# The attention mask of a four-layer graph kernel: TensorE's mask products or an addition on VectorE

## The chip, the cores and the metric

The kernel runs on one core of one Trainium2 chip. Its engines are TensorE (PE, with its weight loads as PEld), VectorE (DVE), ScalarE (ACT), GpSimd (POOL) and SyncE (SP, which issues DMAs here). The metric is the device time of one execution in microseconds (us), lower is better.

## The reference

Input are 128 graphs of 64 nodes with 256 features (`x`, float32) and one 64x64 adjacency matrix `adj` of zeros and ones. Four graph layers follow one another, each with a residual and a layer norm: x = layernorm(x + layer(x)).

- Layer 0 is graph attention of one head, masked by multiplication with `adj`.
- Layer 1 is a graph convolution, `adj @ x @ weight + bias`.
- Layer 2 is attention with 8 heads of 32, a projection and an inner layer norm. Its core:

```python
attn = jnp.einsum('bhnd,bhmd->bhnm', q, k) * scale
attn = jnp.where(attn_mask[None, None] == 0, -jnp.inf, attn)
attn = jax.nn.softmax(attn, axis=-1)
o = jnp.einsum('bhnm,bhmd->bhnd', attn, v)
```

- Layer 3 is a gated recurrent layer of three steps, each with two aggregations over the graph, gates z and r, a candidate, and an update of h.

## The kernel before, in words

The 8192 rows are cut into 16 units of 512 rows (8 graphs, four tiles of 128 rows; two graphs share a tile). The kernel is a software pipeline over all layers, written out by hand. Each engine has one stream, `body(i)`, that runs for i from -4 to 16 (2 to 11 as a loop on the chip, the rest written out). In pass i the engine works on layer 3 of unit i, on most of layer 2 of unit i + 1, on layer 1 and the first part of layer 2 of unit i + 2, and on layer 0 of unit i + 3. The order inside `body` is the order on the engine; a `Signal` is a semaphore on which one engine waits for a count of another's work. Nothing reorders the parts.

PSUM is two groups of four banks of 512 float32: `X` holds gates and candidates of layer 3 (`RZ` and `HV`), `Y` all of the layers 0 to 2. Large products are made of three float32r products each (`matmul3`, L109 to L111). In the trace all banks are called `banks`; `l_prob` is `l2_prob`, `l_mx` is `l2_mx`, `l_qk` is `l2_qk`, and `l_h`, `l_r`, `l_rh_hi` and `l_rh_lo` belong to layer 3. `l_qk` also receives the transposed probabilities.

The change is in the masked softmax of layer 2, at the start of each pass:

- TensorE, `l2_mask` (L592): it waits for the four copies of q and k to SBUF (`l2_qk_ready`, ScalarE, L908) and for the copies of v (L847). Then, for each of four banks, one bf16 product of the identity with the broadcast mask writes 0 or -3e38 into all 512 columns.
- TensorE, `l2_score` (L603): 128 small products of 32x64 accumulate onto the mask. Heads lie in four groups of 32 rows, and each group has a bank.
- VectorE, `l2_max` (L1290) and `l2_shift` (L1298): four times a maximum over the 64 nodes of each head, read from the bank, and four times the bank less that maximum, written to `b.prob` in SBUF.
- ScalarE, `l2_exp` (L928): four exponentials, in place, in `b.prob`. The first waits for all four shifts.
- TensorE, `l2_turn_prob` (L614): sixteen transposes, four for each exponential. They write into the banks of the scores.
- ScalarE, `l2_take_prob` (L847, out `l_qk`): four copies to SBUF. TensorE, `l2_attend` (L629): 64 small products with v, each quarter after its copy.

Between the scores and the transposes TensorE has five parts of layer 3, `l3_u` twice, `l3_r` twice and `l3_w` once: 30 products of 512 columns. Between transposes and attend it has `l3_diff(i, 0, 0)`, six more. After attend come `l3_w(i, 0, 1)` and `l3_candidate(i, 0, 0)`, which needs `b.rhs` (L1148, `l_rh_lo`) from VectorE. VectorE does the eight softmax instructions first in its pass, right behind `l1_add_bias` (L1256) of the pass before, and then `l3_reset` (L1381). ScalarE has `l3_reset(i, 0, 0)` (L971) before the exponentials and `l3_reset(i, 0, 1)` and a copy (`l3_high_rh`) between the copies of the probabilities. The last TensorE part of a pass is `l3_turn` (L727), which transposes the new h (L1405). `l1_residual` is L1268, `l0_residual` is L1236.

```python
def body(i):                 # VectorE, start of a pass
    l2_max(i + 1, 0)
    l2_max(i + 1, 1)
    l2_shift(i + 1, 0)
    l2_max(i + 1, 2)
    l2_shift(i + 1, 1)
    l2_max(i + 1, 3)
    l2_shift(i + 1, 2)
    l2_shift(i + 1, 3)
    l3_reset(i, 0, 0)
```

Of the kernel before, what the change touches and what calls it, by code (L numbers as in the profile page):

```python
# [7 lines left out]
BF16 = mybir.dt.bfloat16  # L8
ALU = mybir.AluOpType
# [3 lines left out]
GRAPHS, NODES, DIM = 128, 64, 256  # L13
P = 128
PER_TILE = P // NODES
TILES = 4
GROUP = TILES * P
UNITS = GRAPHS * NODES // GROUP
CH = DIM // P
HEADS, HD = 8, 32  # L20
ROWS = P // HD
# [12 lines left out]
class Signal:  # L34


    def __init__(self, p, name, per):
        self.sem, self.per = p.sem(name), per
# [34 lines left out]
class Program:  # L73
    def __init__(self, nc, a, out, stack):
        self.nc, self.a, self.out, self.stack = nc, a, out, stack
        self.taken = []
        self.ps = [stack.enter_context(nc.psum_tensor(f"banks{s}", [P, TILES, BANK], F32)) for s in (0, 1)]
        sb = self.sb
        self.ident = sb("ident", [P, P])
        self.ident_bf = sb("ident_bf", [P, P], BF16)  # L80
        self.adj_t = sb("adj_t", [P, P])
        self.adj2 = sb("adj2", [P, NODES])
        self.mask_bias = sb("mask_bias", [P, NODES], BF16)
        self.nan_rows = sb("nan_rows", [P, 1])
        self.same_graph = sb("same_graph", [P, P])
        self.ident2 = sb("ident2", [P, NODES])
        self.eps = sb("eps", [P, TILES])
        self.minus_half = sb("minus_half", [P, TILES])
        self.const_ready = self.sem("const_ready")

    def sb(self, name, shape, dt=F32, stack=None):
        return (stack or self.stack).enter_context(self.nc.sbuf_tensor(name, shape, dt))
# [33 lines left out]
def constants(p, block, own, first_load):  # L126
    nc = p.nc
# [32 lines left out]
    @block.vector  # L160
    def _(dve):
        links = Links(dve, chain)
        dve.wait_ge(loaded, 64)
        dve.wait_ge(made, 1)
        for b in range(PER_TILE):
            q = slice(b * NODES, (b + 1) * NODES)
            nc.vector.memset(p.same_graph[q, q], 1.0)
        nc.vector.tensor_copy(p.ident_bf[:, :], p.ident[:, :])
        nc.vector.tensor_tensor(p.ident2[:, :], p.ident[:, 0:NODES], p.ident[:, NODES:P], ALU.add)
        nc.vector.tensor_scalar(p.mask_bias[:, :], p.adj2[:, :], 0.0, MASKED, ALU.is_equal, ALU.mult)  # L170

        links.link(nc.vector.tensor_scalar(hits[:, :], p.adj2[:, :], 0.0, None, ALU.not_equal))
        links.link(nc.vector.reduce_sum(count[:, :], hits[:, :], AX.X))
        links.link(nc.vector.tensor_scalar(count[:, :], count[:, :], 1.0, None, ALU.min))
        links.link(nc.vector.reciprocal(count[:, :], count[:, :]))
        links.link(nc.vector.tensor_scalar(p.nan_rows[:, :], count[:, :], 0.0, None, ALU.mult))
        dve.wait_ge(turned, 1)
        links.link(nc.vector.tensor_copy(p.adj_t[:, :], p.ps[0][:, 0, 0:P]))
        links.link(nc.vector.tensor_copy(hits[:, 0:1], p.nan_rows[:, :]))
        nc.vector.memset(count[:, :], 0.0).then_inc(p.const_ready, 1)  # L180
# [140 lines left out]
class Signals:  # L321
    def __init__(self, p):
        one = lambda name, per: Signal(p, name, per)
# [15 lines left out]
        self.l2_turned, self.l2_hi, self.l2_lo = one("l2_turned", CH), one("l2_hi", CH), one("l2_lo", CH)  # L339
        self.l2_qk_done, self.l2_qk_ready = one("l2_qk_done", 2 * CH), one("l2_qk_ready", 2 * CH)  # L340
        self.l2_v_done, self.l2_v_staged, self.l2_v_swapped = one("l2_v_done", 1), one("l2_v_staged", 2), one("l2_v_swapped", 32)
        self.l2_scored, self.l2_maxed, self.l2_shifted = one("l2_scored", ROWS), one("l2_maxed", ROWS), one("l2_shifted", ROWS)
        self.l2_exp, self.l2_prob_turned, self.l2_prob_t = one("l2_exp", TILES), one("l2_prob_turned", TILES), one("l2_prob_t", TILES)
        self.l2_pv_done, self.l2_inv, self.l2_o = one("l2_pv_done", TILES), one("l2_inv", 2), one("l2_o", 1)
# [20 lines left out]
def fused(p, block, w, b, s, norms, src, dst):  # L365
# [6 lines left out]
    nc = p.nc  # L372
    X, Y = p.ps
# [90 lines left out]
    def _(pe):  # L464
# [120 lines left out]
            ins.then_inc(s.l2_v_done.sem, 1)  # L585

        @within
        def l2_mask(u):
            pe.wait_ge(*s.l2_qk_ready.at(u, 2 * CH))
            pe.wait_ge(*s.l2_v_staged.at(u, 2))  # L590
            for r in range(ROWS):
                nc.tensor.matmul(Y[:, r, :], p.ident_bf[:, :],  # L592
                                 p.mask_bias[:, :].unsqueeze(1).to_broadcast([P, TILES * CH, NODES]),
                                 start=True, stop=False, skip_group_check=True)

        @within
        def l2_score(u, t):
            for c in range(CH):
                for n in range(PER_TILE):
                    for r in range(ROWS):  # L600
                        q = slice(t * P + n * NODES, t * P + (n + 1) * NODES)
                        col = (t * CH + c) * NODES
                        ins = nc.tensor.matmul(  # L603
                            Y[n * NODES:(n + 1) * NODES, r, col:col + NODES],
                            b.qk[r * HD:(r + 1) * HD, c, q], b.qk[r * HD:(r + 1) * HD, CH + c, q],
                            start=False, stop=True, skip_group_check=True)
                        if (t, c, n) == (TILES - 1, CH - 1, PER_TILE - 1):
                            ins.then_inc(s.l2_scored.sem, 1)

# [125 lines left out]
            aggregate(HV[:, k, :], b.h_tok, k).then_inc(s.adj_done.sem, 1)  # L735

        def body(i):
            l2_mask(i + 1)
            l2_score(i + 1, 0)
            l2_score(i + 1, 1)  # L740
            l2_score(i + 1, 2)
            l2_score(i + 1, 3)
            l3_u(i, 0, 0)
# [363 lines left out]
    def _(dve):  # L1107
# [39 lines left out]
        def lower(parts, k, bank):  # L1147
            return nc.vector.tensor_tensor(parts[1][:, k, :], bank, parts[0][:, k, :].bitcast(F32), ALU.subtract)  # L1148
# [134 lines left out]
        def l2_low(u, k):  # L1283
            dve.wait_ge(*s.l2_hi.at(u, k + 1))
            lower(b.late, k, Y[:, 2 + k, :]).then_inc(s.l2_lo.sem, 1)

        @within
        def l2_max(u, r):
            dve.wait_ge(*s.l2_scored.at(u, r + 1))
            nc.vector.tensor_reduce(b.mx[:, r, :], Y[:, r, :].rearrange("p (n j) -> p n j", j=NODES),  # L1290
                                    AX.X, ALU.max).then_inc(s.l2_maxed.sem, 1)

        @within
        def l2_shift(u, r):
            dve.wait_ge(*s.l2_maxed.at(u, r + 1))
            by_bank = b.prob[:, :, :, :].rearrange("p t (c r) j -> p t c r j", c=CH)
            m = b.mx[:, r, :].rearrange("p (t c) -> p t c", t=TILES).unsqueeze(3).to_broadcast([P, TILES, CH, NODES])
            nc.vector.tensor_tensor(by_bank[:, :, :, r, :], Y[:, r, :].rearrange("p (t c j) -> p t c j", t=TILES, c=CH),  # L1298
                                    m, ALU.subtract).then_inc(s.l2_shifted.sem, 1)

        @within
# [126 lines left out]
        l3_offset = within(lambda u: l3.take_offset(dve, u))  # L1428

        def body(i):  # L1430
            l2_max(i + 1, 0)
            l2_max(i + 1, 1)
            l2_shift(i + 1, 0)
            l2_max(i + 1, 2)
            l2_shift(i + 1, 1)
            l2_max(i + 1, 3)
# [149 lines left out]
```

## Time and profile before

| | |
|---|---|
| median of three runs | 1490.17 us (1487.84 to 1492.82) |
| the profiled execution | 1487.55 us |
| its span, first to last instruction | 1485.5 us |
| instructions | 26652 |
| mean granted TensorE clock | 0.961 of full speed |
| data moved by DMA | 34.62 MB, 23 GB/s on average |

The profile is of one execution. A row of the timeline has the start in us from the span's start, the duration, the engine, the line of the kernel, the operation with output and inputs, the shape, a count where neighbours of one kind are merged, and in brackets the idle time of the engine in front of it with what ended it. TensorE's products are pipelined, so the duration of one is longer than the distance to the next start.

### The profile page before, as it was taken

The page shows a single profiled execution, that of the slowest core. Times are in us where ns is not written, and L with a number is a line of the kernel's source. Part 1 is how long each engine was busy: PE and PEld are TensorE (multiplying, and loading weights), DVE is VectorE, ACT ScalarE, POOL GpSimd, SP SyncE. Part 2 cuts the span into 40 slices and gives each one's busy share as a digit, 9 for nine tenths or more (in the row PEclk, how much of TensorE's full clock was granted, in tenths as well). Part 3 has the DMA queues.
Part 4 walks back from the last instruction along what each step waited for, and adds up shares of the span by engine and source line. Part 5 has one row for each costly group of instructions (what it writes and reads, how often), then busy time and mean ns, then how long its engine had stood idle before and what let it go on. Part 6 is the DMA issues. An engine that isn't in the chain of part 4 may idle for free.

```text
span 1485.5 us, 26652 instructions
## 1 busy us (share of the span) xinstructions
PE 1365.8 (92%) x10357; PEld 1153.5 (78%) x10357; DVE 1058.4 (71%) x2366; ACT 794.1 (53%) x1450; POOL 146.5 (10%) x196
## 2 busy tenths in 40 slices
PE   3566799999999999999999999999999999999885
PEld 2455688888888888888888888888888888878674
DVE  3455587777778787777778787777778787757444
ACT  1342455566656555565656555565656555555433
POOL 4300001110001011110001011110001001100000
PEclk8677799999999999999999999999999999999998
DMA  4000100000000000000000000001000000001000
GB/s 136 15 22 1 36 1 23 29 15 23 15 21 28 21 28 21 28 14 23 12 21 28 21 28 21 28 14 28 7 21 28 22 29 8 29 1 37 1 29 15
DMA packets 54661, 34.62 MB, mean 23 GB/s; under 512 B 34896, under 2 KB 51536, under 8 KB 54608
## 3 DMA queue, kind: packets, MB, share of 16 engines
q1 hardware_dynamic: 52800, 29.43, 6.7%
q0 software_dynamic: 1248, 3.94, 0.8%
q8 instruction: 36, 0.59, 0.2%
q10 hardware_dynamic: 560, 0.52, 0.1%
q14 instruction: 17, 0.14, 0.0%
HBM read 12.92 MB, written 8.39 MB: 14 GB/s over the span
## 4 chain that ended last, share of the span: by engine, by line
PE 67%; DVE 17%; ACT 8%; issue 4%; POOL 2%; DMA 0%; ACTq 0%; SPq 0%; POOLq 0%; DVEq 0%
PE banks L109 16%; PE banks L110 15%; PE banks L111 15%; PE banks L485 8%; PE banks L480 3%; PE banks L537 2%; PE banks L629 2%; ACT y L284 2%; PE banks L614 2%; PE banks L603 2%; DVE l_stats L256 2%; DVE l_r L1399 1%; ACT banks L982 1%; ACT l_qk L908 1%; DVE late_lo L1148 1%
## 5 line engine op out<-in xcount | busy, mean ns | idle before, releaser
L971 ACT ACTIVATE l_r<-banks,bias_r 128x512 f32<-128x512 f32 x96 | 65.9, 686 | 223.3 <-PE banks L111 223.3
L270 POOL TENSOR_TENSOR l_rstd<-l_mv,eps 128x4 f32<-128x4 f32 x48 | 28.3, 589 | 949.3 <-DVE l_mv L264 949.3
L988 ACT ACTIVATE banks<-banks,bias_h 128x512 f32<-128x512 f32 x96 | 63.3, 659 | 59.7 <-PE banks L111 59.6
L1148 DVE TENSOR_TENSOR l_rh_lo<-l_r,l_rh_hi 128x512 fp32r<-128x512 f32 x96 | 66.0, 688 | 36.6 <-ACT l_rh_hi L847 36.3
L1399 DVE SCALAR_TENSOR_TENSOR l_r<-banks,l_r 128x512 f32<-128x512 f32 x96 | 66.0, 687 | 32.1 <-ACT banks L982 29.2
L1381 DVE SCALAR_TENSOR_TENSOR l_r<-l_r,l_h 128x512 f32<-128x512 f32 x64 | 43.6, 682 | 55.4 <-ACT l_r L971 55.4
L284 ACT ACTIVATE y<-l_sum,l_offset,l_rstd 128x256 f32<-128x256 f32 x128 | 70.6, 591 | 19.0 <-DVE l_offset L278 19.0
L109 PE MATMUL banks<-l_rh_hi,u_hi 128*128 128x512 f32 x192 | 78.2, 408 | 0.0
L485 PE MATMUL banks<-adj_t,y 128*128 128x128 f32 x512 | 67.7, 282 | 10.9 <-ACT y L284 9.9
L982 ACT ACTIVATE banks<-banks,bias_z 128x512 f32<-128x512 f32 x96 | 63.5, 662 | 25.9 <-PE banks L111 25.9
L110 PE MATMUL banks<-l_rh_hi,u_lo 128*128 128x512 f32 x192 | 75.7, 394 | 0.0
L111 PE MATMUL banks<-l_rh_lo,u_hi 128*128 128x512 f32 x192 | 75.6, 394 | 0.0
L485 PEld LDWEIGHTS banks<-adj_t,y 128*128 128x128 f32 x512 | 62.4, 196 | 15.0 <-ACT y L284 10.6
L485 PE MATMUL banks<-adj_t,l_htok 128*128 128x128 f32 x512 | 67.2, 287 | 3.7 <-ACT l_htok L847 3.7
L485 PEld LDWEIGHTS banks<-adj_t,l_htok 128*128 128x128 f32 x512 | 62.4, 199 | 9.8 <-ACT l_htok L847 9.8
L908 ACT ACTIVATE l_qk<-banks 128x512 f32<-128x512 f32 x64 | 38.3, 599 | 51.9 <-PE banks L111 50.1
L727 PE MATMUL banks<-ident,l_h 128*128 128x128 f32 x384 | 50.9, 276 | 13.2 <-DVE l_h L1405 13.2
L847 ACT ACTIVATE l_rh_hi<-l_r 128x512 fp32r<-128x512 f32 x96 | 60.7, 632 | 4.0 <-DVE l_r L1381 4.0
L284 ACT ACTIVATE y<-l_sum,l2o_offset,l2o_rstd 128x256 f32<-128x256 f32 x64 | 33.3, 591 | 52.3 <-DVE l2o_offset L278 52.3
L1381 DVE SCALAR_TENSOR_TENSOR l_r<-l_r,f_h 128x512 f32<-128x512 f32 x32 | 22.2, 692 | 53.0 <-ACT l_r L971 52.4
L284 ACT ACTIVATE l_res<-l_res,l_offset,l_rstd 128x256 f32<-128x256 f32 x64 | 36.2, 596 | 41.8 <-DVE l_offset L278 41.8
L727 PEld LDWEIGHTS banks<-ident,l_h 128*128 128x128 f32 x384 | 44.1, 142 | 17.7 <-DVE l_h L1405 15.8
(238 smaller groups left out, 4370.9 us busy)
## 6 DMA issues: line engine op xcount, KB each, us to landing
x_tok<-in_x_dram SPq DMA_DIRECT2D x16, 512.0 KB, 3.8
l_res<-y SPq DMA_DIRECT2D x16, 512.0 KB, 2.9
out_dram<-l_res SPq DMA_DIRECT2D x16, 512.0 KB, 2.9
l_vpair<-l_vstage SPq DMA_DIRECT2D x32, 128.0 KB, 3.1
w_raw<-in_L_gnn_w_w_dram POOLq DMA_DIRECT2D x3, 512.0 KB, 9.7
qkv_raw<-in_L_gnn_w_qkv_dram POOLq DMA_DIRECT2D x1, 768.0 KB, 7.4
u_raw<-in_L_gnn_u_w_dram POOLq DMA_DIRECT2D x2, 256.0 KB, 9.7
l_w_raw<-in_L_gnn_W_dram ACTq DMA_DIRECT2D x1, 256.0 KB, 4.8
```

The costliest lines, as they stand in the source:

```text
L109: nc.tensor.matmul(out, w[0], x[0], start=first, stop=False, skip_group_check=True)
L110: nc.tensor.matmul(out, w[1], x[0], start=False, stop=False, skip_group_check=True)
L111: return nc.tensor.matmul(out, w[0], x[1], start=False, stop=last, skip_group_check=True)
L284: return self.p.nc.scalar.activation(y[:, t, :], z[:, t, :], ACT.Identity, scale=self.rstd[:, t:t + 1], bias=self.offset[:, t:t + 1])
L485: ins = nc.tensor.matmul(bank[:, columns(t)], tokens[:, t, k * P:(k + 1) * P], p.adj_t[:, :], start=True, stop=True)
L727: ins = nc.tensor.transpose(RZ[:, n, t * DIM + k * P:t * DIM + (k + 1) * P], b.l3_h[:, k, columns(2 * n + t)], p.ident[:, :])
L971: nc.scalar.activation(b.r[:, m, :], RZ[:, m, :], ACT.Tanh, scale=0.5, bias=w.biases["r"][:, m:m + 1]).then_inc(s.r_ready.sem, 1)
L982: nc.scalar.activation(RZ[:, m, :], RZ[:, m, :], ACT.Tanh, scale=0.5, bias=w.biases["z"][:, m:m + 1]).then_inc(s.z_ready.sem, 1)
L988: nc.scalar.activation(HV[:, m, :], HV[:, m, :], ACT.Tanh, bias=w.biases["h"][:, m:m + 1]).then_inc(s.hv_ready.sem, 1)
L1148: return nc.vector.tensor_tensor(parts[1][:, k, :], bank, parts[0][:, k, :].bitcast(F32), ALU.subtract)
L1381: nc.vector.scalar_tensor_tensor(b.r[:, m, :], b.r[:, m, :], 1.0, h_before(step)[:, m, :], ALU.add, ALU.mult).then_inc(s.rh.sem, 1)
L1399: nc.vector.scalar_tensor_tensor(b.r[:, m, :], RZ[:, m, :], 1.0, b.r[:, m, :], ALU.add, ALU.mult).then_inc(s.step.sem, 1)
```

## The change

The mask goes from TensorE to VectorE, in all units. The four mask products go; the wait in front of them stays as `l2_wait_to_score`, and the score products start their banks' regions themselves. VectorE gets `l2_add_mask`: for each bank it adds the mask, broadcast over tiles and heads and now held in float32, and writes the sum to `b.prob`. Maximum and shift then read `b.prob` instead of the bank. The bf16 identity goes from the set-up. VectorE's written order has the four additions between the maxima.

```diff
-        self.ident_bf = sb("ident_bf", [P, P], BF16)
-        self.mask_bias = sb("mask_bias", [P, NODES], BF16)
+        self.mask_bias = sb("mask_bias", [P, NODES])
...
-        nc.vector.tensor_copy(p.ident_bf[:, :], p.ident[:, :])
...
+        self.l2_masked = one("l2_masked", ROWS)
...
-        def l2_mask(u):
+        def l2_wait_to_score(u):
             pe.wait_ge(*s.l2_qk_ready.at(u, 2 * CH))
             pe.wait_ge(*s.l2_v_staged.at(u, 2))
-            for r in range(ROWS):
-                nc.tensor.matmul(Y[:, r, :], p.ident_bf[:, :],
-                                 p.mask_bias[:, :].unsqueeze(1).to_broadcast([P, TILES * CH, NODES]),
-                                 start=True, stop=False, skip_group_check=True)
...
                             b.qk[r * HD:(r + 1) * HD, c, q], b.qk[r * HD:(r + 1) * HD, CH + c, q],
-                            start=False, stop=True, skip_group_check=True)
+                            start=True, stop=True, skip_group_check=True)
...
         def body(i):
-            l2_mask(i + 1)
+            l2_wait_to_score(i + 1)
...
+        by_bank = b.prob[:, :, :, :].rearrange("p t (c r) j -> p t c r j", c=CH)
+
+        @within
+        def l2_add_mask(u, r):
+            dve.wait_ge(*s.l2_scored.at(u, r + 1))
+            over = p.mask_bias[:, :].unsqueeze(1).unsqueeze(1).to_broadcast([P, TILES, CH, NODES])
+            nc.vector.tensor_tensor(by_bank[:, :, :, r, :], Y[:, r, :].rearrange("p (t c j) -> p t c j", t=TILES, c=CH),
+                                    over, ALU.add).then_inc(s.l2_masked.sem, 1)
+
         @within
         def l2_max(u, r):
-            dve.wait_ge(*s.l2_scored.at(u, r + 1))
-            nc.vector.tensor_reduce(b.mx[:, r, :], Y[:, r, :].rearrange("p (n j) -> p n j", j=NODES),
+            dve.wait_ge(*s.l2_masked.at(u, r + 1))
+            nc.vector.tensor_reduce(b.mx[:, r, :].rearrange("p (t c) -> p t c", t=TILES), by_bank[:, :, :, r, :],
                                     AX.X, ALU.max).then_inc(s.l2_maxed.sem, 1)
...
-            nc.vector.tensor_tensor(by_bank[:, :, :, r, :], Y[:, r, :].rearrange("p (t c j) -> p t c j", t=TILES, c=CH),
+            nc.vector.tensor_tensor(by_bank[:, :, :, r, :], by_bank[:, :, :, r, :],
                                     m, ALU.subtract).then_inc(s.l2_shifted.sem, 1)
...
         def body(i):
+            l2_add_mask(i + 1, 0)
+            l2_add_mask(i + 1, 1)
             l2_max(i + 1, 0)
+            l2_add_mask(i + 1, 2)
             l2_max(i + 1, 1)
             l2_shift(i + 1, 0)
+            l2_add_mask(i + 1, 3)
             l2_max(i + 1, 2)
             l2_shift(i + 1, 1)
             l2_max(i + 1, 3)
```

## Rows read from the trace of the kernel before

**Rows 1.** The page, busy time of each engine, share of the span, instructions.

```profile
PE 1365.8 (92%) x10357; PEld 1153.5 (78%) x10357; DVE 1058.4 (71%) x2366; ACT 794.1 (53%) x1450; POOL 146.5 (10%) x196
```

**Rows 2.** Stretches: one pass; columns PE, PEld, DVE, ACT, POOL, PEclk, DMA, GB/s.

```profile
423.81:507.26 83.45, 82.69 (x646) 70.18 (x647) 64.98 (x147) 48.98 (x90) 7.79 (x10) 1.00 0.07 22
```

**Rows 3.** Waits of TensorE: waiter, releaser, total us, times, longest.

```profile
PE banks L727 <- DVE l_h L1405: 13.2, 6, 2.2
...
PE banks L592 <- ACT l_qk L908: 12.0, 15, 2.5
...
PE banks L614 <- ACT l_prob L928: 5.6, 1, 5.6
```

**Rows 4.** Timeline of TensorE from 423 to 441 us, a unit in the loop.

```profile
423.81 1.03 PE L592 MATMUL banks<-mask_bias,ident_bf 128*128 128x512 bf16 x4 [0.68 <-ACT l_qk L908]
424.78 1.59 PE L603 MATMUL banks<-l_qk 32*64 32x64 f32 x128
...
433.40 1.91 PE L614 MATMUL banks<-ident,l_prob 128*128 128x128 f32 x16
435.06 0.48 PE L109 MATMUL banks<-f_a_hi,diff_hi 128*128 128x512 f32 x1
...
436.64 2.10 PE L629 MATMUL banks<-l_vpair,l_qk 128*64 128x66 f32 x64
...
440.17 0.39 PE L109 MATMUL banks<-l_rh_hi,u_hi 128*128 128x512 f32 x1
```

**Rows 5.** Timeline of VectorE in the same unit.

```profile
426.60 1.28 DVE L1290 TENSOR_REDUCE l_mx<-banks 128x8 f32<-128x512 f32 x2
...
430.19 1.28 DVE L1298 TENSOR_TENSOR l_prob<-banks,l_mx 128x512 f32<-128x512 f32 x2
...
437.74 0.69 DVE L1148 TENSOR_TENSOR l_rh_lo<-l_r,l_rh_hi 128x512 fp32r<-128x512 f32 x1 [0.90 <-ACT l_rh_hi L847]
```

**Rows 6.** Timeline of ScalarE in the same unit.

```profile
431.50 2.19 ACT L928 ACTIVATE l_prob<-l_prob 128x512 f32<-128x512 f32 x4
434.03 0.60 ACT L847 ACTIVATE l_qk<-banks 128x512 f32<-128x512 f32 x1 [0.34 <-PE banks L614]
...
435.62 1.57 ACT L847 ACTIVATE l_qk<-banks 128x512 f32<-128x512 f32 x3
```

**Rows 7.** Single lines of VectorE: count, duration in ns min/median/max, starts, shape.

```profile
L1268 DVE TENSOR_TENSOR l_sum<-banks,l_sum x32: 681/690/692, 53.5 to 1297.6; 128x512 f32<-128x512 f32 x32
...
L1236 DVE SCALAR_TENSOR_TENSOR l_sum<-l_v,x_tok x32: 682/683/684, 34.7 to 1242.9; 128x512 f32<-128x512 f32 x32
```

**Rows 8.** Timeline of VectorE, first maximum of units 1 and 15.

```profile
176.06 1.29 DVE L1290 TENSOR_REDUCE l_mx<-banks 128x8 f32<-128x512 f32 x2 [5.78 <-PE banks L603]
...
1341.59 1.29 DVE L1290 TENSOR_REDUCE l_mx<-banks 128x8 f32<-128x512 f32 x2 [0.19 <-PE banks L603]
```

**Rows 9.** Timeline of TensorE from 1378 to 1435 us.

```profile
1378.55 0.66 PE L480 MATMUL banks<-ident,y 128*128 128x128 f32 x4 [2.99 <-ACT y L284]
...
1391.04 3.78 PE L485 MATMUL banks<-adj_t,l_htok 128*128 128x128 f32 x16 [0.74 <-ACT l_htok L847]
...
1434.02 2.05 PE L485 MATMUL banks<-adj_t,l_htok 128*128 128x128 f32 x16 [0.74 <-ACT l_htok L847]
```

**Rows 10.** Stretches of 8 us late in the kernel, columns as in rows 2.

```profile
1308.00:1316.00 8.00, 5.83 (x30) 5.27 (x31) 4.54 (x13) 4.29 (x8) 1.56 (x2) 0.79 0.00 0
1376.00:1384.00 8.00, 5.45 (x36) 4.98 (x37) 3.94 (x7) 6.72 (x13) 0.11 (x1) 1.00 0.00 1
1388.00:1396.00 8.00, 6.05 (x28) 5.53 (x29) 3.62 (x6) 3.08 (x6) 0.00 (x0) 0.65 0.00 0
1412.00:1420.00 8.00, 6.87 (x26) 5.57 (x27) 2.73 (x7) 0.00 (x0) 0.00 (x0) 0.79 0.00 0
1432.00:1440.00 8.00, 7.07 (x42) 6.09 (x43) 2.81 (x5) 3.89 (x7) 0.00 (x0) 1.00 0.24 88
1452.00:1460.00 8.00, 7.05 (x42) 6.05 (x43) 2.83 (x5) 2.80 (x5) 0.00 (x0) 1.00 0.00 0
```

More of the change, by code:

```diff
@@ L1295, in l2_shift @@
             dve.wait_ge(*s.l2_maxed.at(u, r + 1))
-            by_bank = b.prob[:, :, :, :].rearrange("p t (c r) j -> p t c r j", c=CH)
             m = b.mx[:, r, :].rearrange("p (t c) -> p t c", t=TILES).unsqueeze(3).to_broadcast([P, TILES, CH, NODES])
-            nc.vector.tensor_tensor(by_bank[:, :, :, r, :], Y[:, r, :].rearrange("p (t c j) -> p t c j", t=TILES, c=CH),
+            nc.vector.tensor_tensor(by_bank[:, :, :, r, :], by_bank[:, :, :, r, :],
                                     m, ALU.subtract).then_inc(s.l2_shifted.sem, 1)
```

## The prediction, made before the changed kernel was built

> **What bounds the kernel now.** I began with the page's shares: TensorE is busy for 92% of the span, VectorE for 71%, ScalarE for 53% [rows 1]. That names TensorE, but VectorE and ScalarE feed it, so the second question is where they are late. The table by stretches shows how even the middle is: one pass of the loop (one unit of 512 rows in each layer) takes 83.45 us, TensorE busy for 82.7 of them, VectorE for 65.0, at full granted clock [rows 2]. So in the middle nearly every microsecond added to or taken from TensorE's stream is a microsecond of the span. The list of waits then says what interrupts it at this place: the mask products wait for the last copy of q and k (12.0 us in 15 waits), and the transposes of the probabilities wait once, 5.6 us, for the exponentials [rows 3]. Once in sixteen units: in the other fifteen the softmax chain on VectorE and ScalarE is covered by gate products. How well it is covered decides this case, and only the order of time tells that.
>
> I read one unit of the loop in the three timelines. **TensorE** starts the mask products at 423.81, the scores at 424.78, works through thirty gate products, starts the sixteen transposes at 433.40 and is at its next gate product at 435.06, at attend at 436.64 [rows 4]. **VectorE** comes to its first maximum at 426.60 without an idle time in front of it, that is from other work, the bias addition of layer 1, and not from a wait for the scores; its eight instructions (four maxima, four shifts) end at 430.19 + 1.28 = 431.47 [rows 5]. **ScalarE** starts the four exponentials at 431.50 and ends them at 433.69 [rows 6].
>
> **Removed.** The four mask products hold TensorE from 423.81 to 424.78: 0.97 us a unit. The wait for q and k in front of them stays, as the scores need the same copies. The copy of the identity to bf16 in the set-up goes too, one small VectorE instruction outside the loop: nothing, beside the waits for the loads. The mask in float32 takes its one set-up instruction as before. A first score product with start instead of accumulate has the same shape: nothing, and I know no row that would price it otherwise. No DMA is moved or added.
>
> **Added.** Four additions of 128x512 from PSUM and SBUF to SBUF. The nearest row is the residual of layer 1, which adds a bank and an SBUF tile of that size: 690 ns; an instruction of the same size with both tensors in SBUF has 683 ns [rows 7]. What counts is the distance of starts: from 426.60 to 431.47 there are eight instructions, the last lasting 0.68, so (4.87 - 0.68) / 7 = 0.60 us each. Four more are 2.40 us. The maxima and shifts now read SBUF; I take the same 0.60, since the two rows differ by 7 ns. The written order puts at least one other instruction between an instruction and the one that it waits for, as before, so the new waits for the masked sums are over when reached. As ends I keep -0.06 us for the eight instructions that now read SBUF (eight times 7 ns) and +0.7 us, should each of the eight take its whole 690 ns of duration instead of a distance of 0.60. I take the middle of the engine's habit, 0.60, because eight neighbours of the same size keep it.
>
> The Trainium skill's page VectorE: DVE Perf Modes, in the section on the TRN2 errata, puts a fixed 120 cycles on an instruction that reads PSUM and 58 on one that reads SBUF. By that the eight instructions would be 62 cycles each, some 0.5 us in all, cheaper, an estimate from that page, and it speaks for the change; the trace does not agree, with 690 against 683 ns.
>
> **Where the path moves.** Does VectorE start earlier because the scores are done 0.97 us earlier? In the usual unit it does not: it comes from other work at 426.60 either way [rows 5]. So the last shift ends at 431.47 + 2.40 = 433.87, the first exponential (0.616 us, from 2.19 us for four at a distance of 0.525) is done at 434.52, the last at 433.69 + 2.40 = 436.09. TensorE, now 0.97 early, is ready for the transposes at 432.43. It waits until about 434.58 (I allow 0.06 us for the hand-over; from VectorE to ScalarE it is 0.03, 431.47 to 431.50 [rows 5, 6]), that is 2.15 us, and then goes at the exponentials' pace. The last four transposes start at 436.15 and take 4/16 of 1.66 us, so the next gate product starts at 436.57 instead of 435.06: **1.51 us later**. Put otherwise: the old order had 0.95 us of slack for the last exponential (433.69, first needed at 434.64); dropping the mask products uses it up, and the added 2.40 us are then nearly all exposed.
>
> What is late next? ScalarE's copies of the transposed probabilities: before, the first started at 434.03 and the last three ran from 435.62 to 437.19 [rows 6], a queue of 3.16 us with two steps of layer 3 in it. They now follow the exponentials, from about 436.1 to 439.3, and attend's last quarter would be reached at 436.64 + 1.51 + 1.5 = 439.65: covered by 0.35 us. The first reset gate's product on VectorE, queued behind the chain, is 2.40 us later; its low half is needed at 440.17 [rows 4] and ended at 437.74 + 0.69 = 438.43 [rows 5], now 440.8 against a need at 441.7: covered. Everything after that is released by attend and moves with TensorE. At the end of the pass the wait for q and k follows copies that are released by TensorE's own products, so it moves too and gives nothing back.
>
> **The other units.** Units 2 to 14 are thirteen like this: 13 x 1.51 = 19.6. Their chain starts 2.79 us after q and k are ready (426.60 - 423.81), and scores are done at 2.56 now, at 1.6 then. In unit 1 VectorE waited 5.78 us for the scores [rows 8], so its chain will start at 1.6, 1.2 before the usual, and the unit loses only 0.3. In unit 15 that wait is 0.19 us, so its chain starts at about 2.3, 0.5 before the usual: it loses 1.0. Unit 0 has nothing beside the chain, which is 2.40 - 0.97 = 1.4 longer. Together 19.6 + 0.3 + 1.0 + 1.4 = **22.3 us**.
>
> **The clock.** Inside the loop TensorE has no stop of over 1 us now. Late in the kernel it has six waits of 2.2 us for the new h [rows 3] and one of 2.99 us [rows 9]; the last of the six, at 1472 us, has no dense work behind it and is left out. In stretches of eight microseconds that begin at or shortly before such a wait's end, the granted clock is 0.79, 0.65 and 0.79 after the waits that ended near 1309, 1389 and 1412 us, which is some time at 1.2 GHz within 2.4 GHz; it stays at 1.00 after those near 1432 and 1452 and after the one of 2.99 us, at 1378.55 [rows 10]. Three of six, then. The same sixteen products take 3.78 us at the low clock and 2.05 at the high one [rows 9], so a fall costs up to 1.7 us on dense work. The new stop is about as long, 2.15 us, but has no second wait of 0.74 us close behind, as two of the three that fell had. I take fewer than half: 4 of 13. And 1.4 us each, since part of the slow time will lie where TensorE goes at the exponentials' pace anyway: **5.6 us**. The ends are none, and all thirteen at 1.7, which is 22.1.
>
> **The sum** stands against the profiled execution: 1487.55 us, of which the span is 1485.5. 1487.55 + 22.3 + 5.6 = 1515.5. The median of the runs shown is 1490.17, 2.6 us above it, so the forecast is **1518 us**.
>
> **Rivals.** (A) The chain stays covered, and only the mask products count: 16 x 0.97 = 15.5 us less, 1474.7. The place is the first transpose; the point of decision is an added chain of 0.95 us, where loss and saving cancel. It needs four additions at under 0.24 us each, or VectorE free a good deal sooner. Nothing of this size runs that fast here; 6%, and 3% more for a partial cover that ends within 0.3%, about what a measurement of this kernel can tell from no change. (B) The mechanism as forecast, but the clock never falls: 1490.17 + 22.3 = 1512.5. For it stand the three waits without a fall; 24%. (C) The clock falls at nearly every new stop: 1490.17 + 22.3 + 22.1 = 1534.6; 14%. (D) TensorE's lateness is partly made up at the end of the pass, because the copies of q and k are then in time: the 0.68 us wait goes, 13 x 0.68 = 8.8 less than B, near 1503.7. Against it: those copies are released by TensorE's last products; 8%. The forecast has 45%.
>
> On B there is a rule. The Trainium skill's page TensorE: Matmul & The Clock Gate, in the section Why this matters for your kernels, says that the clock is lost by idle gaps of over about 3 us. By that rule the stop of 2.15 us would cost nothing more and the time would be B's 1512.5; the trace disagrees in part, with falls behind waits of 2.20 us and none behind 2.99.
>
> **Range and chances.** 1505 to 1533 holds the forecast, B, part of C (the clock falling at up to twelve stops) and a third of D. Slower by over 0.3% 0.91, within 0.3% 0.03, faster 0.06.
>
> **What would show it.** Right: in the changed kernel's loop a wait of some 2.1 us in front of the transposes of L614 for the exponentials, thirteen times; the VectorE chain of twelve instructions at 0.60 us; a pass of 85.0 us where the clock stays at 1.00 and 1.4 us more where it falls; scores straight behind the wait for q and k. Wrong: no wait before the transposes, a start of the first addition well before 2.8 us after q and k are ready, reductions from SBUF much shorter than 0.68 us, or a pass of the same length with a shorter wait at its end. A new long wait at attend or at the candidate's products would mean that I took the copies' slack too large.

## The result and the profile after

The changed kernel takes 1519.59 us (median of four runs, 1518.02 to 1521.57) against 1489.01 for the kernel before (the three runs of the table above and one more): the ratio is 1.0203, with a 95% interval from 1.0178 to 1.0229. The forecast was 1518 us. The profiled execution took 1519.06 us, its span is 1517.0, which is 31.5 more than before.

The page's shares first, to be held against [rows 1]:

```profile
PE 1366.6 (90%) x10293; PEld 1156.5 (76%) x10293; DVE 1094.1 (72%) x2429; ACT 793.3 (52%) x1450; POOL 146.5 (10%) x196
```

TensorE has 64 products fewer and yet no less busy time, since it ran longer at the low clock (mean granted clock 0.955 against 0.961). VectorE has 35.7 us more, for 64 additions that stand about 0.60 us apart. Neither number tells 31.5 us. The list of TensorE's waits shows where to look; its first and last line here stood at 5.6 and 12.0 us in [rows 3]:

```profile
PE banks L609 <- ACT l_prob L923: 35.5, 16, 7.9
PE banks L722 <- DVE l_h L1408: 13.2, 6, 2.2
...
PE banks L598 <- ACT l_qk L903: 12.2, 15, 2.5
```

The wait of the transposes for the exponentials occurs in all sixteen units now. The wait for q and k in front has stayed as it was. One unit in the loop, TensorE, to be held against [rows 4]:

```profile
513.21 1.59 PE L598 MATMUL banks<-l_qk 32*64 32x64 f32 x128 [0.69 <-ACT l_qk L903]
...
521.60 0.40 PE L110 MATMUL banks<-f_a_lo,w5s_hi 128*128 128x512 f32 x1
523.96 2.22 PE L609 MATMUL banks<-ident,l_prob 128*128 128x128 f32 x16 [1.96 <-ACT l_prob L923]
525.93 0.48 PE L108 MATMUL banks<-f_a_hi,diff_hi 128*128 128x512 f32 x1
...
527.52 2.09 PE L624 MATMUL banks<-l_vpair,l_qk 128*64 128x66 f32 x64
```

VectorE in the same unit, to be held against [rows 5]:

```profile
515.99 1.28 DVE L1288 TENSOR_TENSOR l_prob<-banks,mask_bias 128x512 f32<-128x512 f32 x2
517.19 0.68 DVE L1294 TENSOR_REDUCE l_mx<-l_prob 128x8 f32<-128x512 f32 x1
517.78 0.68 DVE L1288 TENSOR_TENSOR l_prob<-banks,mask_bias 128x512 f32<-128x512 f32 x1
...
521.96 1.28 DVE L1301 TENSOR_TENSOR l_prob<-l_prob,l_mx 128x512 f32<-128x512 f32 x2
```

And ScalarE, to be held against [rows 6]:

```profile
523.28 2.19 ACT L923 ACTIVATE l_prob<-l_prob 128x512 f32<-128x512 f32 x4 [3.35 <-DVE l_prob L1301]
525.38 0.57 ACT L842 ACTIVATE l_qk<-banks 128x512 f32<-128x512 f32 x1
```

Counted from the moment when q and k are ready (513.21), VectorE starts its chain at 2.78 us, as before at 2.79, ends it at 10.03 instead of 7.66, and the first gate product behind the transposes starts at 12.72 instead of 11.25: 1.47 us later.

Stretches of one pass each, the first with a fall of the clock, the second without, then the end of the kernel from unit 15's scores (columns as in [rows 2]):

```profile
342.02:428.27 86.25, 83.60 (x642) 71.47 (x643) 67.19 (x151) 48.97 (x90) 7.79 (x10) 0.98 0.07 23
428.27:513.21 84.94, 82.19 (x642) 69.78 (x643) 67.18 (x151) 48.85 (x90) 7.79 (x10) 1.00 0.07 22
...
1363.77:1517.00 153.23, 122.57 (x737) 100.70 (x736) 80.92 (x166) 60.78 (x104) 6.75 (x10) 0.88 0.06 20
```

A pass is 84.94 us, 1.49 more than 83.45, and about 1.35 more again in four passes. In those the granted clock is at its 1.2 GHz level for 3.4 us, beginning at 352.8, 694.2, 950.2 and 1206.2 us, that is right behind the new wait. In eight-microsecond stretches it looks like this, with a pass without a fall as the second line:

```profile
350.00:358.00 8.00, 6.13 (x38) 5.12 (x38) 4.38 (x13) 6.02 (x12) 0.98 (x2) 0.79 0.00 0
...
521.00:529.00 8.00, 6.04 (x77) 4.65 (x77) 4.44 (x12) 5.72 (x12) 0.69 (x2) 1.00 0.00 0
692.00:700.00 8.00, 6.21 (x64) 5.51 (x66) 3.96 (x11) 6.39 (x12) 1.21 (x2) 0.79 0.00 0
948.00:956.00 8.00, 6.05 (x59) 5.50 (x60) 4.15 (x12) 6.40 (x12) 1.21 (x2) 0.79 0.00 0
1204.00:1212.00 8.00, 5.98 (x55) 5.38 (x56) 4.26 (x12) 6.41 (x12) 1.21 (x2) 0.79 0.01 2
```

The 31.5 us of the two spans, by stretches between the points at which a unit's q and k are ready: up to unit 0, +0.2; from unit 0 to 1, 77.84 against 78.05, -0.2; from 1 to 2, 83.68 against 83.44, +0.2; the thirteen passes from unit 2 to 15, 1106.67 against 1082.14, +24.5; from unit 15 to the end, 153.23 against 146.46, +6.8.

### The profile page after: what moved, and what is told of

Its sections match the earlier page's. It is cut to its first block, busy times and chain, and to the rows that moved or that the text cites. A ratio compares the mean times of both kernels' runs of the same rounds, so it can differ in the third digit from the quotient of the medians.

```text
span 1517.0 us, 26587 instructions
## 1 busy us (share of the span) xinstructions
PE 1366.6 (90%) x10293; PEld 1156.5 (76%) x10293; DVE 1094.1 (72%) x2429; ACT 793.3 (52%) x1450; POOL 146.5 (10%) x196
## 4 chain that ended last, share of the span: by engine, by line
PE 73%; DVE 19%; issue 3%; ACT 3%; DMA 0%; POOL 0%; DVEq 0%; SPq 0%; POOLq 0%; ACTq 0%
PE banks L108 18%; PE banks L110 17%; PE banks L109 17%; PE banks L484 8%; PE banks L479 3%; PE banks L609 3%; DVE l_mx L1294 3%; DVE l_prob L1301 2%; PE banks L536 2%; PE banks L624 2%; DVE l_prob L1288 2%; PE banks L722 2%; DVE l_r L1402 1%; DVE l_res L1426 1%; DVE l_stats L254 1%
## 5 line engine op out<-in xcount | busy, mean ns | idle before, releaser
L609 PE MATMUL banks<-ident,l_prob 128*128 128x128 f32 x256 | 42.2, 326 | 35.5 <-ACT l_prob L923 35.5
L484 PE MATMUL banks<-adj_t,l_htok 128*128 128x128 f32 x512 | 70.5, 296 | 3.6 <-ACT l_htok L842 3.6
L484 PEld LDWEIGHTS banks<-adj_t,l_htok 128*128 128x128 f32 x512 | 65.7, 208 | 9.9 <-ACT l_htok L842 9.9
L609 PEld LDWEIGHTS banks<-ident,l_prob 128*128 128x128 f32 x256 | 34.1, 164 | 45.7 <-ACT l_prob L923 42.2
L923 ACT ACTIVATE l_prob<-l_prob 128x512 f32<-128x512 f32 x64 | 35.1, 618 | 57.5 <-DVE l_prob L1301 57.5
```

Of the source, the lines that this page charges most:

```text
L484: ins = nc.tensor.matmul(bank[:, columns(t)], tokens[:, t, k * P:(k + 1) * P], p.adj_t[:, :], start=True, stop=True)
L609: ins = nc.tensor.transpose(Y[:, t, columns(g)], b.prob[:, t, 2 * g:2 * g + 2, :].rearrange("p h j -> p (h j)"), p.ident[:, :])
```

## The experiments

All are compared with the kernel before, run on the same chip beside them; its median was 1489.67 us beside e1 to e4, 1490.47 beside e5 to e7 and 1492.41 beside e8 to e11. "Pass" is the distance of two units' score parts in the loop.

**The removal alone (e1_no_mask).** The kernel before without its mask products and without any addition.

```diff
-            for r in range(ROWS):
-                nc.tensor.matmul(Y[:, r, :], p.ident_bf[:, :],
-                                 p.mask_bias[:, :].unsqueeze(1).to_broadcast([P, TILES * CH, NODES]),
-                                 start=True, stop=False, skip_group_check=True)
...
-                            start=False, stop=True, skip_group_check=True)
+                            start=True, stop=True, skip_group_check=True)
```

> Edit: the kernel before without the four mask products, and no addition on VectorE; the mask of layer 2 is left out of the computation. Theory 1 (TensorE's stream sets the pass, the softmax chain is just covered): the pass gets 0.97 us shorter, 83.45 to about 82.5, the transposes wait next to nothing (under 0.1 us), and the time is about 1489.0 - 15.5 = 1473.5 us. Rival (the wait for q and k in front sets the pass, so that shorter TensorE work only lengthens it): pass 83.45 with a wait of 1.65 us instead of 0.68, time 1489 us.

Measured: 1478.97 us, ratio 0.9926 (0.9900 to 0.9952). The pass is 82.63 us, 0.82 less than before.

```profile
417.71:500.34 82.63, 81.85 (x643) 69.91 (x643) 64.79 (x147) 48.88 (x90) 7.80 (x10) 1.00 0.07 22
```

The wait for q and k is 0.68 us as before, so the rival fell. The removal is worth nearly its time as long as the chain is covered. It is 10.7 us in all instead of 15.5, which hides two differences outside the loop: the stretch from unit 0 to 1 is 74.36 us instead of 78.05, and the end is longer. From the start of unit 15's scores to the last instruction it takes 151.33 us, against 1485.5 - 1340.01 = 145.5 for the kernel before, at a granted clock of 0.88 instead of 0.92. More on the end below; the shorter start was not followed up.

**Both costs together (e2_zero_products).** The changed kernel, with four bf16 products of the identity and a tile of zeros where the mask products were.

```diff
+            for r in range(ROWS):
+                nc.tensor.matmul(Y[:, r, :], p.ident_bf[:, :],
+                                 p.zero_mask[:, :].unsqueeze(1).to_broadcast([P, TILES * CH, NODES]),
+                                 start=True, stop=False, skip_group_check=True)
...
-                            start=True, stop=True, skip_group_check=True)
+                            start=False, stop=True, skip_group_check=True)
```

> Edit: the changed kernel with four products of the bf16 identity and a tile of zeros where the mask products were, so that both costs are there and the result is the same. Theory 1 (the loss is exposed chain, so what TensorE does before the transposes is free): the pass stays 84.94 us, the wait before the transposes falls from 1.96 to 1.0 us, time as the changed kernel or up to 5 us less, should the shorter wait no longer lower the clock: 1514 to 1520 us. Rival (removal and addition are two separate terms, each worth its time): 15.5 us more than the changed kernel, 1535 us.

Measured: 1517.01 us, ratio 1.0187 (1.0158 to 1.0216), 2.6 us *less* than the changed kernel's median. Its pass is 84.97 us, and the wait takes up the products' time (timeline of TensorE):

```profile
512.92 1.03 PE L595 MATMUL banks<-zero_mask,ident_bf 128*128 128x512 bf16 x4 [0.69 <-ACT l_qk L911]
513.89 1.59 PE L606 MATMUL banks<-l_qk 32*64 32x64 f32 x128
...
523.68 2.22 PE L617 MATMUL banks<-ident,l_prob 128*128 128x128 f32 x16 [1.00 <-ACT l_prob L931]
```

So in the changed kernel the removal of the mask products is worth nothing, though alone it was worth 10.7 us: what TensorE saves in front of the transposes it waits. With a wait of 1.00 us instead of 1.96 no pass of the loop has a fall of the clock.

**An earlier chain (e3_bias_later).** The changed kernel; VectorE's bias addition of layer 1 goes behind the first reset product.

```diff
             l3_reset(i, 0, 0)
+            l1_add_bias(i + 2)
             l3_reset(i, 0, 1)
...
-            l1_add_bias(i + 3)
```

> Edit: the changed kernel, with VectorE's addition of the bias of layer 1 (1.12 us from start to next start) moved from in front of the softmax chain to behind the first reset product. Theory 1 (the start of the chain on VectorE sets the stall): the chain starts 1.7 instead of 2.78 us after the scores' start, the wait before the transposes falls from 1.96 to 0.9 us, the pass from 84.94 to 83.85, and with no fall of the clock in the loop the time is 1519.6 - 13 x 1.1 - 5.3 = 1500 us. Rival (VectorE has become the bound by its work, wherever it is placed): no change, 1519.6 us. Rival 2 (something between chain and transposes, the exponentials or the banks, sets it): pass unchanged at 84.94.

Measured: 1497.33 us, ratio 1.0049 (1.0031 to 1.0066). The chain starts at 510.97 - 509.32 = 1.65 us (first line, VectorE), the wait is 0.85, the pass 83.79, and no pass of the loop has a fall:

```profile
510.97 1.27 DVE L1288 TENSOR_TENSOR l_prob<-banks,mask_bias 128x512 f32<-128x512 f32 x2
...
509.32:593.11 83.79, 82.17 (x643) 69.71 (x643) 67.11 (x151) 48.83 (x90) 7.78 (x10) 1.00 0.07 22
```

VectorE's work is the same to 0.1 us (67.11 against 67.18), so its amount is not the bound; its order is. This gives back 22 of the 30 us without taking anything away.

**Dense work in the wait (e4_filler).** The changed kernel, with six products issued twice.

```diff
             l3_w(i, 0, 0)
+            l3_w(i, 0, 1)
             l2_turn_prob(i + 1, 0)
```

> Edit: the changed kernel, with the six gate products of l3_w(i, 0, 1) issued once more in front of the transposes, 1.40 us of dense work that the later, original six overwrite. Theory 1 on time and clock (the wait is idle time, and its idleness makes the clock fall at some passes): the pass stays 84.94 us, the wait falls from 1.96 to 0.56 us, no pass of the middle has a fall, and four passes lose their 1.35 us: about 1514 us. Rival (the falls in the loop don't come from this wait): falls as before, 1519.6 us. Rival 2 (TensorE's work is the bound in every pass): 1.4 us more in each of 15 passes, 1540 us.

Measured: 1516.53 us, ratio 1.0173 (1.0146 to 1.0201), 3 us less than the changed kernel with 1.4 us more work in each unit. The pass stays 84.94:

```profile
513.14 1.59 PE L598 MATMUL banks<-l_qk 32*64 32x64 f32 x128 [0.70 <-ACT l_qk L904]
...
523.88 2.22 PE L609 MATMUL banks<-ident,l_prob 128*128 128x128 f32 x16 [0.55 <-ACT l_prob L924]
```

No pass of the loop has a fall, against four in the changed kernel. This shows that the four falls belong to the new wait: with six more products in it and nothing else changed they are gone. That only 3 of the expected 5.3 us come back has to do with the end: the pass from unit 14 to 15 is 83.46 us against 82.17, with a fall of 6.8 us in the old waits instead of 3.4, and the rest of the kernel is 0.8 us longer.

**Two more additions (e6_two_more).** The changed kernel with two unused additions of 128x512 behind the last maximum.

```diff
             l2_max(i + 1, 3)
+            l2_again(i + 1, 0)
+            l2_again(i + 1, 1)
             l2_shift(i + 1, 2)
```

> Edit: the changed kernel with two more additions of 128x512 from a bank to SBUF in VectorE's chain, behind the last maximum; nobody uses their results. Theory 1 (the chain is fully exposed, 0.60 us an addition): the pass grows by 1.20 us to 86.14, in units 0 to 15 alike, and the wait before the transposes to 3.16 us; 1519.6 + 16 x 1.2 = 1539 us, and up to 15 us more for more falls of the clock. Rival (the exposed cost is a hand-over or the wait itself, not a count of additions): pass below 85.5, under 1530 us.

Measured: 1559.28 us, ratio 1.0465 (1.0437 to 1.0492). A pass without a fall is 86.14 us, to the digit 1.20 more; the wait is 3.15 us. But of the thirteen passes of units 2 to 14 only one is like this. In the twelve others the clock falls, in eight of them for 6.8 us (a pass without and one with a fall):

```profile
522.77:608.91 86.14, 82.20 (x642) 69.74 (x643) 68.40 (x153) 48.89 (x90) 7.79 (x10) 1.00 0.07 21
962.48:1051.21 88.73, 84.79 (x643) 72.14 (x643) 68.49 (x153) 49.00 (x90) 7.79 (x10) 0.96 0.07 21
```

I had allowed up to 15 us for more falls and it took 20.5: 1519.6 + 19.2 + 20.5 = 1559.3. The count of additions is confirmed, the price of the longer wait was put too low. (The 20.5 us are what the total leaves over. By the profiles, the passes from unit 2 to 15 are 37.05 us longer than in the changed kernel, 13 x 1.20 = 15.6 of it by the additions and the other 21.45 by the clock.)

**The changed kernel again (e7_after_again).** No edit.

> Edit: none; the changed kernel once more, for its second profile. Theory 1 (passes of 84.94 us, 1.35 more where the clock falls, and a tail whose falls come where the waits meet them): the passes of the middle again 84.94 or about 86.3 us, three to five of the latter; the stretch from unit 15's scores to the end differs from the first profile's 153.2 us by up to 5 us. Rival (the falls are fixed by the program): the same four passes and 153.2 us within 0.5.

Measured: 1519.45 us, ratio 1.0196 (1.0171 to 1.0221). In its profile the same passes have the falls (those that begin with units 3, 7, 10 and 13) and the stretch from unit 15's scores to the end is 1516.4 - 1363.22 = 153.2 us again. That lies within the bounds of both, and the rival's were the narrow ones: in two profiles of this kernel the falls of the loop are at the same places.

**The slack of the kernel before, tested from the other side (e9_before_one, e10_before_two).** The kernel before with one and with two unused additions in the chain, the mask still on TensorE. The edit is that of e6_two_more, once or twice, with the float32 adjacency matrix as the second operand.

```diff
             l2_max(i + 1, 3)
+            l2_again(i + 1, 0)
             l2_shift(i + 1, 2)
```

> Edit: the kernel before with one more addition of 128x512 from a bank to SBUF in VectorE's chain behind the last maximum; nobody uses its result. Theory 1 (the last exponential has 0.95 us of slack there): 0.60 us fit into it, the pass stays 83.45 us, and only unit 0 gets 0.6 us longer: 1490 to 1491 us. Rival (every addition on VectorE costs its 0.60 us): pass 84.05, 1499.7 us.

> Edit: the kernel before with two such additions, 1.20 us. Theory 1: the chain outlasts the slack of 0.95 by 0.25 to 0.3 us, so the pass is 83.72 us and the time 15 x 0.27 + 1.2 = 5 us above the kernel before, about 1495 us. Rival (every addition costs 0.60): pass 84.65, 1509 us. Rival 2 (the slack is larger than I read, and something else made the changed kernel slow): pass 83.45, 1490 us.

Measured: 1489.07 us (ratio 0.9985, 0.9971 to 0.9998) with one, 1493.14 us (1.0022, 1.0006 to 1.0038) with two. The medians spread by some us with the end of the kernel, so the passes are the better witness. One pass each, first with one, then with two:

```profile
591.29:674.76 83.47, 82.66 (x648) 70.10 (x647) 65.50 (x148) 48.87 (x90) 7.79 (x10) 1.00 0.07 22
```

```profile
508.63:592.39 83.76, 82.98 (x647) 70.01 (x646) 66.00 (x149) 48.81 (x90) 7.79 (x10) 1.00 0.07 22
```

These are single passes. On average over the twelve from unit 2 to unit 14 a pass takes 83.44 us in the kernel before, 83.48 with one addition and 83.74 with two. The first costs 0.04 us a pass, the second 0.26, where I had expected none and 0.27. In the changed kernel two more cost 1.20. That is the whole case in three numbers: the same instruction is nearly free, partly free or fully paid, by what is left of 0.95 us.

**The kernel before again (e11_before_again).** No edit.

> Edit: none; the kernel before once more, for its second profile. In its first the stretch from unit 15's scores to the end is 140.5 us with the clock low for 10.2 us before the last fall at 1472; in the changed kernel it is 148.2 us in both profiles, where the later transposes account for 1.9 only. Theory 1 (where the falls in the tail come is left to chance, and the first profile of before was a lucky one): the second profile's tail is 143 to 147 us. Rival (the change itself makes the tail's waits worse): 140.5 us again within 1.

Measured: one run of 1485.91 us, with a last stretch of 145.44 us, as before:

```profile
506.63:590.08 83.45, 82.68 (x647) 70.16 (x647) 64.98 (x147) 48.93 (x90) 7.79 (x10) 1.00 0.07 22
1338.46:1483.90 145.44, 116.15 (x737) 95.24 (x736) 77.84 (x160) 60.55 (x104) 6.74 (x10) 0.92 0.06 20
```

By this profile the rival held. (The expectation's 140.5 and 148.2 us are each 5.0 too small: the stretches are 145.49 and 153.23 us. The difference between them is right.) The timed runs say more, however. The 23 of the kernel before beside this one fall into two groups, ten from 1485.85 to 1491.00 us and thirteen from 1492.41 to 1494.45, the second at a mean clock of 0.958 to 0.959, the first at 0.962 to 0.966. And the profile of e9_before_one, whose loop is that of the kernel before to 0.04 us a pass, took 1493.08 us, with this end:

```profile
1340.20:1491.00 150.80, 121.64 (x737) 100.28 (x736) 78.43 (x161) 61.01 (x104) 6.75 (x10) 0.88 0.06 20
```

That is 5.4 us more than the end of e11_before_again, counted from the same part, at the clock of 0.88 that the changed kernel shows there. The difference lies at waits that all these kernels have there, one of 3.0 us and then five of 2.2. Behind the first five of these six the clock is low for 3.4, 3.4, 6.8, 6.8 and 3.4 us in e9_before_one, and for none, 6.8, 3.4, none and none in both profiles of the kernel before. The two groups of times suggest that the kernel before also has executions with the long end, and that its two profiles both caught the short one; no profile of it shows the long one. What decides between the two ends was not tested.

**A version without the wait (e5_reordered, e8_split).** First the changed kernel with the bias addition later, six gate products ahead of the transposes, six others behind them, and on ScalarE the second reset gate ahead of the exponentials.

```diff
             l3_w(i, 0, 0)
+            l3_diff(i, 0, 0)
             l2_turn_prob(i + 1, 0)
...
-            l3_diff(i, 0, 0)
+            l3_w(i, 0, 1)
             l2_attend(i + 1, 0)
...
             l2_attend(i + 1, 3)
-            l3_w(i, 0, 1)
...
             l3_reset(i, 0, 0)
+            l3_reset(i, 0, 1)
             l2_exp(i + 1, 0)
...
             l2_take_prob(i + 1, 0)
-            l3_reset(i, 0, 1)
...
             l3_reset(i, 0, 0)
+            l1_add_bias(i + 2)
             l3_reset(i, 0, 1)
...
-            l1_add_bias(i + 3)
```

> Edit: the changed kernel reordered. VectorE's bias addition of layer 1 behind the first reset product; on TensorE l3_diff(i, 0, 0) in front of the transposes and l3_w(i, 0, 1) between transposes and attend; on ScalarE l3_reset(i, 0, 1) in front of the exponentials. Theory 1: the wait before the transposes is gone (ready at 10.0 us after the scores' start, first exponential at 9.65, last at 11.2 for a need at 11.26), so the pass is 83.45 - 0.97 = 82.5 us plus up to 0.5 for a late low half of the reset product at the candidate; time 1474 to 1482 us, under both kernels. Rival (a wait of the same size comes up behind, at attend or at the candidate's products): pass 83.9 us or more, 1495 us or more.

Measured: 1491.69 us, ratio 1.0006 (0.9994 to 1.0017), no change against the kernel before. The wait in front of the transposes is gone, but a new one stands a few us later (timeline of TensorE):

```profile
507.32 1.59 PE L598 MATMUL banks<-l_qk 32*64 32x64 f32 x128 [0.70 <-ACT l_qk L903]
...
517.34 1.91 PE L609 MATMUL banks<-ident,l_prob 128*128 128x128 f32 x16
...
520.59 2.09 PE L624 MATMUL banks<-l_vpair,l_qk 128*64 128x66 f32 x64
...
524.94 1.09 PE L479 MATMUL banks<-ident,l_otok 128*128 128x128 f32 x8 [0.67 <-DVE l_otok L1319]
```

I had looked for the new wait at attend or at the candidate's products. It is at the transposes of the attention output: by moving l3_w(i, 0, 1) in front of attend I had halved what covers VectorE's division behind attend. The second version splits those six products; `l3_w` now takes as its last argument which half it issues:

```diff
-            l3_w(i, 0, 1)
+            l3_w(i, 0, 1, (0,))
             l2_attend(i + 1, 0)
...
             l2_attend(i + 1, 3)
+            l3_w(i, 0, 1, (1,))
```

> Edit: e5_reordered with l3_w(i, 0, 1) split in two: three products (0.70 us) between transposes and attend, three behind attend. In e5_reordered the pass was 83.36 us, with a new wait of 0.67 us for the attention output (l_otok) in front of its transposes. Theory 1 (that wait is what took e5_reordered's expected gain, since only six products instead of twelve cover VectorE's work on the output): the wait is gone, the copies of the probabilities are still in time, the pass is 82.7 us, and the time about 1491.7 - 14 x 0.67 = 1482 us. Rival (the wait moves to attend, because the copies are late, or to the candidate): pass 83.2 us or more, 1490 us.

Measured: 1481.92 us, ratio 0.9939 (0.9920 to 0.9958): 0.6% faster than the kernel before and 37.7 us under the changed kernel, with the mask on VectorE all the same. No wait is left in this part:

```profile
504.26 1.59 PE L598 MATMUL banks<-l_qk 32*64 32x64 f32 x128 [0.68 <-ACT l_qk L906]
...
514.28 1.91 PE L609 MATMUL banks<-ident,l_prob 128*128 128x128 f32 x16
...
516.83 2.09 PE L624 MATMUL banks<-l_vpair,l_qk 128*64 128x66 f32 x64
...
521.23 1.09 PE L479 MATMUL banks<-ident,l_otok 128*128 128x128 f32 x8
```

Its pass is 82.66 us, 0.79 less than before and within 0.03 us of the pass without any mask (82.63 in e1_no_mask), so next to nothing of the four additions is exposed. The kernel before in this new order was not run, so how much of the 0.6% the order alone would give there is open.

## Why the prediction was right

**The price of the additions: right.** Forecast were twelve instructions at a distance of 0.60 us, 2.40 more. The chain went from 4.87 to 7.25 us, 2.38 more. The maxima and shifts hardly changed by reading SBUF: the median maximum went from 681 to 676 ns, the shift from 680 to 681. The Trainium skill's page VectorE: DVE Perf Modes, in the section on the TRN2 errata, has 58 fixed cycles for a source in SBUF against 120 in PSUM; a saving of that size did not appear.

**The start of the chain and the slack: right.** The chain began 2.78 us after q and k were ready, against 2.79, so VectorE gained nothing from earlier scores. The slack of 0.95 us, read from the row of the transposes and the end of the exponentials, was confirmed from both sides: one more addition costs 0.04 us a pass in the kernel before, the second 0.26. The loss in a usual pass was 1.49 us for a forecast of 1.51, and the wait 1.96 for 2.15.

**The removal: right.** It is worth 0.82 us a pass by itself (e1_no_mask) and nothing beside the additions (e2_zero_products). Rival A, the covered chain, is what e1_no_mask and e8_split show: it needs not cheaper additions but an earlier start and other products in front of the transposes.

**What is late next: right.** Attend follows with its usual distance (14.31 against 12.72, 1.59 us, as 12.83 against 11.25, 1.58 us, before), and the wait for q and k at the pass's end is still there, 0.69 us against 0.68, so rival D is out.

**The clock in the loop: right in kind, its count by luck.** Forecast were four falls of 1.4 us; there were four, of 1.35 us each. That it was exactly four is more than the reasoning could give: it had three of six cases and a guess downwards. The reason given for the guess, no second wait close behind, doesn't hold in the rows: the waits of 2.2 us near 1432 and 1452 us have a second one of 0.74 us behind them too, and the clock stayed. Nor does the wait of 2.99 us always stay without a fall: in both profiles of the changed kernel and in e9_before_one the clock is low for 3.4 us at its end. Rivals B and C are out. On the rule of the Trainium skill's page TensorE: Matmul & The Clock Gate, section Why this matters for your kernels, gaps of over about 3 us: here waits of 1.9 to 2.0 us, followed by transposes at the exponentials' pace, were enough in four passes of thirteen, and waits of 1.0 us or less in the loop never. The page's bound is too wide for this case.

**The two ends: wrong, and they cancel in part.** For unit 0 I forecast +1.4 us; the stretch from unit 0 to 1 got 0.2 us shorter. The later start of attend was there (13.31 us after q and k instead of 11.93, and 2.1 us more up to the transposes of the attention output), but the low-clock stretches behind it came out shorter: the mean granted clock in that stretch is 0.76 against 0.72.

For unit 15 I forecast +1.0 and the end got 6.8 us longer. The late transposes are 1.0 of it, as forecast: the next gate product starts 12.22 us after q and k instead of 11.26. The other 5.8 us lie at the waits that were there before, one of 3.0 us and five of 2.2. The five distances between these six are 12.20, 21.40, 21.07, 22.73 and 22.82 us instead of 10.66, 22.88, 20.10, 20.02 and 20.08, with the clock low for 3.4, 3.4, 6.8, 6.8 and 6.8 us in them instead of none, 6.8, 3.4, none and none; 0.7 us come back behind the last. The step that failed is the term for the clock, which I had drawn up for the new waits only. The old waits late in the kernel were in my rows with their clock, three of the six I counted with a fall; I took them as given, though which of them have a fall differs from run to run of nearly the same program, as e9_before_one shows beside the kernel before.

So the sum of 27.9 us had 19.6 + 5.6 = 25.2 for the thirteen passes, and they measured 24.5; 0.3 for unit 1, measured 0.2; 2.4 for the two ends, measured 6.8 with the start of the span and unit 0 at zero. Together 27.9 was 3.6 us too little against the profiled execution. That the forecast of 1518 us is still within 1.6 us of the median has luck in it: I added 2.6 us for the distance of the median from the profiled execution, and for the changed kernel that distance is 0.5 us. Against the medians the change is 30.6 us, and in 13 of the 23 later runs of the kernel before the time lies in the longer of the two groups above.

## What to carry to other kernels

In a software pipeline whose main engine never stops, read the slack of each hand-over from one unit's timelines, as need minus readiness, before moving work between engines: work on the feeding chain is free up to that slack and fully paid beyond it, and work taken from the main engine in front of the hand-over uses the slack up. When a move makes a hand-over late, look at what the feeding engine does just before its chain and which products of the main engine can stand in front: here the changed kernel's instructions in another order turned +2.0% into -0.6%. And count what each moved part had covered at its old place.

## What the runs showed of the hardware

- In the loop the granted TensorE clock fell to its lower level behind waits of 1.9 to 2.0 us in four of thirteen passes, behind waits of 3.15 us in twelve of thirteen, and behind none of 1.0 us or less. A fall of 3.4 us cost 1.35 us in the changed kernel (1.0 to 1.5 in e6_two_more), and one of 6.8 us 2.6 (88.73 against 86.14).
- The same wait can have a fall or not. Behind the wait of 3.0 us late in the kernel the clock stayed in both profiles of the kernel before and was low for 3.4 us in both of the changed kernel.
- More work in a wait saved time here: six products that nobody uses took the falls out of the loop and 3 us out of the kernel.
- Executions of the kernel before differed by up to 8.6 us (1485.85 to 1494.45). Two profiles with passes equal to 0.04 us on average (e9_before_one and e11_before_again) differ by 5.4 us in the last 150. For effects of 0.3% of a kernel the length of a pass is the better measure than the total.
- Which passes of the changed kernel have a fall was the same in both profiles. The reason was not tested.
